# Quantised stage: the clip at six as one VectorE instruction, gate times value on GpSimd; the shifted norm's statistics made in attention

## The reference, cut to what matters

```python
def fake_quant_nvfp4(x, global_scale):
    xb = x.reshape(sh[:-1] + (sh[-1] // BLOCK, BLOCK))
    amax = jnp.max(jnp.abs(xb), axis=-1, keepdims=True)
    sc = jnp.clip(amax / FP4_MAX * global_scale, 0.0, FP8_MAX)
    sc8 = sc.astype(jnp.float8_e4m3fn).astype(jnp.float32)
    dq = sc8 / global_scale
    ...
    a = jnp.clip(jnp.abs(xb) / safe_dq, 0.0, FP4_MAX)
    q = jnp.sign(xb) * _FP4_VALS[jnp.digitize(a, _FP4_MIDS)]
    return (q * dq).reshape(sh)

gate_out = nvfp4_linear(x, gate_w, s_in[0])       # 256 -> 1024
up_out = nvfp4_linear(x, up_w, s_in[0])           # 256 -> 1024
hidden = jax.nn.silu(gate_out) * up_out
return nvfp4_linear(hidden, down_w, s_in_down[0]) # 1024 -> 256
```

```python
x = x + o @ wo
h = shift_token(x)
mu = h.mean(-1, keepdims=True)
var = h.var(-1, keepdims=True)
h = (h - mu) / jnp.sqrt(var + 1e-05) * lg + lb
```

## Time and profile before

| | us |
|---|---|
| median of 3 runs | 2471.36 |
| lowest, highest | 2466.46, 2481.22 |
| the profiled execution's own time | 2483.35 |
| its span | 2481.4 |

### The profile page before, as it was taken

How to read it: one execution, slowest core, us unless ns; L and a number is a source line. 1 busy time by engine, 2 the same in 40 slices (tenths; PEclk the granted TensorE clock), 3 DMA queues, 4 the chain that set the end, 5 groups by cost and what they waited for, 6 DMA issues and landing times. The chain is left out here.

```text
span 2481.4 us, 41330 instructions
## 1 busy us (share of the span) xinstructions
PE 2054.0 (83%) x14744; PEld 1484.2 (60%) x14744; DVE 1747.8 (70%) x3765; ACT 1364.9 (55%) x3137; POOL 1038.5 (42%) x1051
## 2 busy tenths in 40 slices
PE   6899999976689997799998888896998886985255
PEld 5344444456566665688886668685877765774123
DVE  6899999855755555776765676766666676568896
ACT  4488888844554444343442347473336565443797
POOL 1322332105534331455553654543535452422554
PEclk9799999987899998899998989998998987997587
DMA  4244444253200001100002000002000001001000
GB/s 111 30 49 52 54 50 49 34 202 128 73 1 1 1 1 59 74 1 1 1 1 88 1 1 2 1 2 95 1 1 1 1 1 39 1 5 56 0 1 34
DMA packets 28489, 80.81 MB, mean 33 GB/s; under 512 B 6016, under 2 KB 19072, under 8 KB 26624
## 3 DMA queue, kind: packets, MB, share of 16 engines
q0 software_dynamic: 10368, 22.38, 7.1%
q1 hardware_dynamic: 17920, 55.80, 6.6%
HBM read 45.07 MB, written 12.06 MB: 23 GB/s over the span
## 5 line engine op out<-in xcount | busy, mean ns | idle before, releaser
L3204 ACT ACTIVATE probs<-psum 128x512 f32<-128x512 f32 (+1 forms) x640 | 344.0, 601 | 97.0 <-PE psum L3128 81.9
L3246 DVE TENSOR_REDUCE max_parts<-psum 128x1 f32<-128x512 f32 x512 | 320.1, 685 | 30.0 <-PE psum L3066 24.3
L328 PE MATMUL psum<-x_upper,weights_upper 128*128 128x512 f32 (+2 forms) x556 | 218.6, 393 | 28.9 <-POOL weights_rest L340 12.7
L340 POOL TENSOR_TENSOR weights_rest<-L1f,weights_upper 128x256 fp32r<-128x256 f32 x216 | 181.7, 868 | 144.7 <-ACT weights_upper L471 144.7
L3128 PE MATMUL psum<-q_stack,k_stack 50*128 50x512 f32 (+1 forms) x640 | 238.4, 457 | 0.2 <-ACT probs L3204 0.2
L328 PE MATMUL psum<-x_rest,weights_upper 128*128 128x512 f32 (+2 forms) x556 | 215.7, 388 | 0.0
L328 PE MATMUL psum<-x_upper,weights_rest 128*128 128x512 f32 (+2 forms) x556 | 214.4, 386 | 0.0
L3066 PE MATMUL psum<-k_stack,q_stack 48*128 48x512 f32 x512 | 194.2, 468 | 12.9 <-ACT probs L3204 7.8
L3138 PE MATMUL psum<-probs,v_tok 128*17 128x256 f32 x2560 | 197.4, 390 | 0.2 <-ACT probs L3204 0.2
L328 PE MATMUL psum<-weights_upper,hidden_upper 128*128 128x256 f32 (+1 forms) x572 | 177.5, 310 | 5.9 <-DVE hidden_rest L340 3.2
L2704 POOL TENSOR_TENSOR probs<-probs,row_sum 128x1024 f32<-128x1024 f32 x64 | 121.0, 1893 | 139.7 <-DVE row_sum L2723 139.7
(11 more groups left out here) (531 smaller groups left out, 6059.1 us busy)
## 6 DMA issues: line engine op xcount, KB each, us to landing
k_stack<-k_parts POOLq DMA_DIRECT2D x56, 147.2 KB, 3.8
L1f<-in_L1f SPq DMA_DIRECT2D x1, 6016.0 KB, 22.2
L2f<-in_L2f SPq DMA_DIRECT2D x2, 2268.0 KB, 8.7
L1x<-in_L1x SPq DMA_DIRECT2D x1, 4226.0 KB
k_stack<-k_parts POOLq DMA_DIRECT2D x56, 73.6 KB, 4.1
L0f<-in_L0f SPq DMA_DIRECT2D x1, 4096.0 KB, 12.3
L2a<-in_L2a SPq DMA_DIRECT2D x2, 2048.0 KB, 13.4
slots_x<-zeros SPq DMA_DIRECT2D x1, 3840.0 KB, 13.3
```

Of the source, the lines that this page charges most:

```text
L328: ins = pe.matmul(out, lhsT(a).bitcast(F32R), rhs(b).bitcast(F32R), start=start and n == 0, stop=stop and n == len(PASSES) - 1, skip_group ...
L340: return engine.tensor_tensor(dst.bitcast(F32R), src, up_part, ALU.subtract)
L3204: act.activation(pb[0:m, n % NPB, (1 - e) * 512:(2 - e) * 512], net.ps[0:m, ST + (2 * n + e) % NS, :], ACT.Exp, scale=HD ** -0.5)\
L3246: ins = v.tensor_reduce(mx3[:, u % 2, a + 4 * e, k:k + 1], src, AX.X, ALU.max)
```

## The change

In the quantised stage:

- `cut_lower`, `cut_upper` and `centre` are gone from ScalarE. `clip`, one `tensor_scalar` with max and min from bf16 to bf16 in SBUF, stands in VectorE's queue, for the first item of a pair behind the second add_up, for the second behind its take_away.
- `hidden` is now a `tensor_tensor` on GpSimd of silu and of the scaled up product. It reads the up product from SBUF: ScalarE gets `scale_up`, which copies it from PSUM with its factor into the new tile `up_scaled` and stands behind each silu. On GpSimd `hidden` of both tiles of pair p+1 stands ahead of divide of pair p.
- The waits follow: largest and silu wait for `hid_ready`, take_away waits for no cut any more.

In the shifted norm:

- The statistics of both halves are made in `local_attend`, tile by tile (`halves_of(t - 3)` between the two take_prev, the last behind the last add_y); their tiles live in `RowStats` for the whole kernel and are filled with the constant once at the start.
- Of the first halves every fourth tile is scaled by ScalarE, with a new small tile `minus_mean_rstd`. The square root's table is loaded at the end of attention's ScalarE queue.

The diff, cut to its core:

```diff
+    def halves(self, v, step, y, t):
+        H2 = D // 2
+        step(v.bn_stats(self.later[:, t, :], y[:, t, H2:D]))
+        step(v.bn_stats(self.both[:, t, 0:6], y[:, t, 0:H2]))
...
         @block.gpsimd
+            def hidden(t):
+                pool.wait_ge(silu_done, t + 1)
+                pool.wait_ge(up_used, t + 1)
+                pool.tensor_tensor(hid[:, t % 4, :], ups[:, t % 2, :], sg[:, t % 2, :], ALU.mult).then_inc(hid_ready, 1)
+
             for p in range(PAIRS + 1):
+                q = p + 1 - HP0
+                if 0 <= q < T // 2:
+                    hidden(2 * q)
+                    hidden(2 * q + 1)
                 if p < PAIRS:
                     divide(2 * p)
                     divide(2 * p + 1)
...
         @block.vector
             def largest(n):
                 if n >= FIRST:
-                    v.wait_ge(up_used, n - FIRST + 1)
+                    v.wait_ge(hid_ready, n - FIRST + 1)
...
-            def hidden(t):
-                v.wait_ge(up_done, t + 1)
-                v.wait_ge(silu_done, t + 1)
-                if t >= 4:
-                    v.wait_ge(ratio_ready, FIRST + t - 3)
-                v.scalar_tensor_tensor(hid[:, t % 4, :], net.ps[:, UP:UP + 2, :].rearrange("p a n -> p (a n)"),
-                                       fac[:, 1:2], sg[:, t % 2, :], ALU.mult, ALU.mult).then_inc(up_used, 1)
...
+            def clip(n):
+                v.wait_ge(minus_ready, n + 1)
+                if n >= 4:
+                    v.wait_ge(out_ready, n - 3)
+                v.tensor_scalar(cut[:, n % 4, :], minus[:, n % 4, :], -FP4_MAX, FP4_MAX, ALU.max, ALU.min)\
+                    .then_inc(cut_ready, 1)
...
                 if p >= 1:
                     take_away(2 * p - 1)
+                    clip(2 * p - 1)
                 for n in (2 * p + 2, 2 * p + 3):
-                    if FIRST <= n < N:
-                        hidden(n - FIRST)
                     if n < N:
                         largest(n)
...
         @block.scalar
-            def cut_lower(n):
-                act.wait_ge(minus_ready, n + 1)
-                act.activation(low12[:, n % 2, :], minus[:, n % 4, :], ACT.Relu, bias=six[:, 0:1])\
-                    .then_inc(cut_below, 1)
...
+            def scale_up(t):
+                act.wait_ge(up_done, t + 1)
+                if t >= 2:
+                    act.wait_ge(hid_ready, t - 1)
+                act.activation(ups[:, t % 2, :], net.ps[:, UP:UP + 2, :].rearrange("p a n -> p (a n)"), ACT.Identity,
+                               scale=fac[:, 1:2]).then_inc(up_used, 1)
...
                 if 0 <= q < T // 2:
                     silu(2 * q)
-                if 0 <= n < N:
-                    for one in (cut_lower, cut_upper, centre):
-                        one(n)
-                if 0 <= q < T // 2:
+                    scale_up(2 * q)
                     silu(2 * q + 1)
-                if 0 <= n < N:
-                    for one in (cut_lower, cut_upper, centre):
-                        one(n + 1)
+                    scale_up(2 * q + 1)
...
 def shifted_norm(net, y, hT, gain, shift, after):
-            pe.wait_ge(own_ready, 1)
...
-            step(v.memset(st[:], float(H2 // 2)))
-            for t in range(T):
-                ins = v.bn_stats(own[:, t, :], y[:, t, H2:D])
-            ins.then_inc(own_ready, 1)
-            step.settle()
-            for t in range(T):
-                step(v.bn_stats(st[:, t, 0:6], y[:, t, 0:H2]))
...
+            v.scalar_tensor_tensor(nb[:], mr[:, :, 0], -1.0, mr[:, :, 1], ALU.mult, ALU.mult).then_inc(nb_ready, 1)
             for t in range(T):
-                v.tensor_scalar(xn[:, t, 0:H2], y[:, t, 0:H2], mr[:, t, 0:1], mr[:, t, 1:2], ALU.subtract,
-                                ALU.mult).then_inc(half_ready[0], 1)
+                if t not in SHARED:
+                    v.tensor_scalar(xn[:, t, 0:H2], y[:, t, 0:H2], mr[:, t, 0:1], mr[:, t, 1:2], ALU.subtract,
+                                    ALU.mult).then_inc(half_ready[0], 1)
...
 def local_attend(net, b, y, lw, qT, kT, vv):
+            if b == B - 1:
+                net.rows.root_table(act)
...
+            def halves_of(t):
+                v.wait_ge(y_taken, t + 1)
+                net.rows.halves(v, step, y, b * WIN + t)
...
                 if 1 <= t <= WIN:
                     take_prev(2 * t - 2)
+                if t >= 3:
+                    halves_of(t - 3)
...
+            halves_of(WIN - 1)
```

More of the change, by code:

```diff
@@ L91, in __init__ @@
         self.warm = net.sb(ctx, "warm", [P, 2])
+        self.both, self.later = net.sb(ctx, "half_stats", [P, T, 12]), net.sb(ctx, "later_half", [P, T, 6])
         self.ve, self.sd, self.rs, self.nb = [net.sb(ctx, name, [P, T]) for name in
@@ L1437, in quantised_ffn @@
         least8 = sb("least8", [P, 2 * NB])
-        six = sb("six", [P, 3])
         big = sb("block_max", [P, 2, 2 * NB])
@@ L1446, in quantised_ffn @@
         minus = sb("minus_rounded", [P, 4, QITEM], BF16)
-        low12 = sb("cut_below", [P, 2, QITEM], BF16)
-        high12 = sb("cut_above", [P, 2, QITEM], BF16)
+        ups = sb("up_scaled", [P, 2, I])
         cut = sb("cut_both", [P, 4, QITEM], BF16)
@@ L1456, in quantised_ffn @@
             sem("ratio"), sem("size"), sem("minus"), sem("cut"), sem("out"))
-        cut_below, cut_above, turned, taken = sem("cut_below"), sem("cut_above"), sem("turned"), sem("taken")
+        hid_ready, turned, taken = sem("hid"), sem("turned"), sem("taken")
         gate_done, up_done, silu_done, up_used, down_done, y_taken = (
@@ L1486, in _ @@
             pool.memset(top8[:], FP8_MAX)
-            pool.memset(least8[:], 1.5 * STEP8 * 2.0 ** -6)
-            pool.memset(six[:, 0:1], FP4_MAX)
-            pool.memset(six[:, 1:2], 2.0 * FP4_MAX)
-            pool.memset(six[:, 2:3], -FP4_MAX).then_inc(constants_ready, 1)
+            pool.memset(least8[:], 1.5 * STEP8 * 2.0 ** -6).then_inc(constants_ready, 1)
             def divide(n):
@@ L1593, in values @@
                 yield
+                clip(2 * p)
+                yield
+            def clip(n):
[4 more added lines that the diff above has]
+                    .then_inc(cut_ready, 1)
             def take(t):
@@ L1702, in measure @@
                 act.activation(size[:, n % 4, :], ratio[:, n % 4, :], ACT.Abs, scale=STEP4).then_inc(size_ready, 1)
-            def cut_lower(n):
-                act.wait_ge(minus_ready, n + 1)
-                act.activation(low12[:, n % 2, :], minus[:, n % 4, :], ACT.Relu, bias=six[:, 0:1])\
-                    .then_inc(cut_below, 1)
-            def cut_upper(n):
-                act.wait_ge(cut_below, n + 1)
-                act.activation(high12[:, n % 2, :], low12[:, n % 2, :], ACT.Relu, bias=six[:, 1:2], scale=-1.0)\
-                    .then_inc(cut_above, 1)
-            def centre(n):
-                act.wait_ge(cut_above, n + 1)
-                if n >= 4:
-                    act.wait_ge(out_ready, n - 3)
-                act.activation(cut[:, n % 4, :], high12[:, n % 2, :], ACT.Identity, bias=six[:, 2:3])\
-                    .then_inc(cut_ready, 1)
+            def scale_up(t):
+                act.wait_ge(up_done, t + 1)
+                if t >= 2:
+                    act.wait_ge(hid_ready, t - 1)
+                act.activation(ups[:, t % 2, :], net.ps[:, UP:UP + 2, :].rearrange("p a n -> p (a n)"), ACT.Identity,
+                               scale=fac[:, 1:2]).then_inc(up_used, 1)
             def take(n):
@@ L1737, in take @@
                 ins.then_inc(taken, 1)
-            act.wait_ge(constants_ready, 1)
             for p in range(PAIRS + 2):
@@ L2257, in shifted_norm @@
     with ExitStack() as ctx:
-        st = net.sb(ctx, "stats", [P, T, 12])
-        own = net.sb(ctx, "later_half", [P, T, 6])
+        st, own = net.rows.both, net.rows.later
+        nb = net.sb(ctx, "minus_mean_rstd", [P, T])
+        SHARED = range(GT - 1, T, GT)
         mv = net.sb(ctx, "mean_var", [P, T, 2])
@@ L2267, in shifted_norm @@
         vec = net.sem(ctx, "sn_vec")
-        own_ready = net.sem(ctx, "own_ready")
+        nb_ready = net.sem(ctx, "nb_ready")
         moved = net.sem(ctx, "stats_moved")
@@ L2274, in shifted_norm @@
         half_ready = [net.sem(ctx, f"half{c}_ready") for c in range(C)]
+        shared_ready = net.sem(ctx, "shared_ready")
         zero_ready = net.sem(ctx, "zero_ready")
@@ L2299, in _ @@
             for n, (c, g) in enumerate(order):
-                pe.wait_ge(half_ready[c], GT * (g + 1))
+                pe.wait_ge(half_ready[c], (GT - 1 if c == 0 else GT) * (g + 1))
+                if c == 0:
+                    pe.wait_ge(shared_ready, g + 1)
                 if n >= 7:
@@ L2355, in _ @@
             act.activation(sd[:], ve[:], ACT.Sqrt).then_inc(sd_ready, 1)
+            act.wait_ge(nb_ready, 1)
+            for t in SHARED:
+                act.activation(xn[:, t, 0:H2], y[:, t, 0:H2], ACT.Identity, bias=nb[:, t:t + 1], scale=mr[:, t, 1:2])\
```

(7 more changed lines are left out.)

3 lines of the change are left out of this document (removed).

## The result

Against the kernel before, run on the same chip, the changed kernel takes **1.0124** times as long, with a 95% interval of 1.0083 to 1.0165: about 31 us more. Its executions took 2505.79, 2507.06 and 2512.13 us; a fourth, of 5516.48 us, was disturbed and counts for nothing, though the median that is shown, 2509.6, is that of four. The profiled one took 2512.13 us.

The account below looks back on a forecast made before the run. VectorE and ScalarE were taken to bound the last stage before the change. Last stage +29.1 us (29.8 + 4.1 - 4.8) and norms -8.6 gave +20.5 on 2471.36: 2492 us, range 2474 to 2508.

Parts of the forecast that it names:

- (a): Last stage, eight pairs with a product on GpSimd: 17.6 us each, 140.8 instead of 111.0 us, +29.8 us.
- the chain: After each second scale-back GpSimd waits 3.8 us for turn, take, silu and scale_up; 15.6 us a pair.
- low-clock case: TensorE's clock at 0.50 in the pairs: turn 1.04 us, second product starting at 7.7 instead of 6.0, pair 18.5 us.
- (b): Early pairs of the last stage: 1.2 us more for each of three, 0.5 for the first, +4.1 us.
- (c): Last stage's tail, last divides to last scale-back's end: 14.7 instead of 19.5 us without six serial cuts, -4.8 us.
- The norms: Two shifted norm stages -9.4 and -1.0 us, statistics at the end of attention +1.8 us, together -8.6 us.
- VectorE no bound: In the last stage's pairs VectorE's next inverse step ends about 5 us ahead of the divide that wants it.
- port waits don't bite: Rival: GpSimd's six steps keep 1.93 us, the eight pairs take 15.6 each; -8 us, 2464 us; chance 0.12.
- The low clock: Rival: TensorE's clock stays low, every pair of the last stage 19.5 to 20 us; +35 us, 2507 us; chance 0.10.
- faster if silu and scale_up came ahead of the takes: Rival: GpSimd's 3.8 us standstill vanishes, VectorE's 11.2 or GpSimd's 11.6 sets the pair; -39 us, 2432 us; chance 0.06.
- exclusion that the forecast relied on: VectorE's two-SBUF-input instructions and GpSimd's take turns whole: add_up 1.15 and small steps 0.2 us more a pair.
- The signs asked for: After profile: GpSimd idle 3.8 us, pairs 17 to 18.5, scale-backs over 2.2, longer add_up and small steps, copy at 1.6.

Follow-up runs that it names:

- experiment 6: Changed kernel with silu and the scaled up product stored in bf16: product 2.12 us, single execution 2511.66 us, last stage 229.9 us.
- experiment 1: Changed norms and attention with the quantised stage of the kernel before: ratio 0.9972 against the kernel before, last stage 195.2 us.
- experiment 4: Changed kernel with both tiles' gate and up products ahead of the turns, silu and scale_up ahead of the takes: ratio 1.0074 against the kernel before.
- experiment 5: Changed kernel with add_up reading one SBUF tile, the addition of the ratio left out: ratio 1.0078 against the kernel before, last stage 216.9 us.

## Why the prediction was right, and where it was short

The direction, and the mechanism by which it comes about, were right; the size was short: +20.5 us against about +31 (21 to 41), and 35.7 in the last stage where 29.1 were forecast. On the 2471.36 us shown, the ratio makes 2502, where 2492 was forecast with a range of 2474 to 2508; the undisturbed executions of the changed kernel have their median at 2507, close to the range's upper end.

- **(a) The pairs with a product: right mechanism, the chain timed too short, one price wrong.** Forecast 17.6 us, measured 18.90 (+40.5 for eight instead of +29.8), just outside the 16.5 to 18.8 of the forecast. By the forecast's own terms, counted from the end of the second scale-back: the second product was to start at 6.0 at the full clock and at 7.7 at the low one, and I took about the middle, 6.85. It starts at 8.05 in the mean (7.84 in seven pairs, 9.5 in the first, whose gate products wait for the take of the gate weights), 1.2 more: it was the low-clock case in nearly every pair. The product was priced at 1.93, as a divide, and takes 2.35, but only the second one's 0.4 lies on the path; the first one's is hidden in the wait for scale_up (experiment 6). The scale-backs lost 0.98 to add_up where 1.15 to 1.35 were counted, 0.3 less. The three together: 17.6 + 1.2 + 0.4 - 0.3 = 18.9. The eight intervals are also not the ones I named: the products stand ahead of the divides one pair earlier, so the last of my eight has none, and the last of my three early ones has them.
- **(b) The early pairs: too high.** Forecast +4.1 for three and the first, measured +1.3 for two and the first: 13.71 instead of 13.16, so 0.55 a pair and not 1.2. The order of waits was right: add_up takes 2.95 behind a scale-back there too. I laid VectorE's instructions behind that wait end to end at their full length, while they start 0.2 (small steps), 0.34 (clip) and 1.14 (large ones) after each other. (a) and (b) together, wherever one cuts: +33.9 forecast, +41.7 measured.
- **(c) The tail: right.** -4.8 forecast, -5.2 measured, with another -0.6 behind it that was not forecast.
- **The norms: right.** -10.4 in the two stages forecast, -12.0 measured; +1.8 in attention forecast, and each of the four calls ends 0.5 to 0.7 us later, some +2.3. Alone they gave -7 (experiment 1; -8.6 forecast). A window of attention still takes 7.51 us, so the 2.06 us of idle time did hide the statistics.
- **VectorE no bound: right for this kernel**, with the inverse step 4.5 us early (forecast 5). With the chain broken up it became the bound at once (experiment 4).

**The rivals.** That port waits don't bite is refuted: experiment 5 takes one operand away and gains 14 us. The low clock (2507, pairs of 19.5 to 20) came nearest by its number, and the start of the second product is that of its case; but the pairs are below it (17.8 to 19.6) and the clock is at 1.00 for a part of each. It was a partner of the mechanism, not another way. That it would be faster if silu and scale_up came ahead of the takes was tried in experiment 4: 16.88 us a pair, where I had priced 11.6. That price came from busy shares and left out the very exclusion that the forecast relied on.

**The signs asked for.** Idle time ahead of the first product, ended by scale_up: 4.3 to 4.6 (7.06 in the first pair), not 3.8. Pairs of 17 to 18.5: 17.8 to 19.6. Scale-backs over 2.2: 2.44. add_up and small steps longer: yes. Copy 1.6 us after the norm's start: 1.3.

## What to carry to other kernels

Before work is moved to an engine that idles, follow what it would wait for, through all queues: here an engine busy half of the time became the longest path, because its new inputs depended on its own last output through TensorE and ScalarE. Moving elementwise work with full operands from VectorE to GpSimd doesn't add a second engine for instructions of VectorE that read two SBUF tiles; count the pair of engines as one for these. And where a cheaper form lengthens the steady state and shortens the tail, use it for the tail only: the clip for the last pair alone kept the gain of 6 us that the clip everywhere gave away again.

## What the runs showed of the hardware that I had not expected

- GpSimd's product of two 128x1024 tiles takes 2.35 us with both operands full f32, 2.12 with both in bf16, and a divide or scale-back, whose second operand is a broadcast one, 1.93. I had taken one price for all.
- The exclusion goes by whole instructions: 0.28 us of work in L1554 takes 2.01 behind a scale-back, and add_up 2.95 instead of 1.22. The clip, which reads one tile in bf16, waits as well: 0.41 alone, 1.16 to 1.18 beside a divide or product. As the Trainium skill ("SBUF — State Buffer", section "Who interferes with whom") has it, the two-port modes of tensor_scalar fall under the rule; these rows agree. The f32 block maxima and the one-operand add_up (1.22 us) don't wait.
- The clip's step of 0.33 to 0.34 us for 1024 bf16 elements agrees with the estimate of 0.35 from "VectorE: DVE Perf Modes" of the Trainium skill (section "Mode 4×_2P — both tricks at once"); the 0.54 that I took from f32 rows was too high.
- Filling TensorE's idle time ahead of the turns (24 matmuls) moved the stretch at the lower clock (1.2 GHz) off the first turn, 0.62 instead of 1.03, but left the second turn (1.04) and the downs (2.6 to 3.6) in it, and gained nothing.
